# Splitting the rotated q and k, and spreading v, on GpSimd instead of ScalarE and VectorE (attention batches 2 to 8)

## The reference

```python
q  = split_heads(layernorm(x) @ Wq, 16)          # 16 heads of 16 features
kv = split_heads(layernorm(x) @ Wkv, 16)         # keys and values are the same tensor
q  = (q * cos + rotate_half(q) * sin) * 16 ** -0.5
kv = kv * cos + rotate_half(kv) * sin
# 8 segments of 64 rows; segment s attends to segments s-1 and s, causally inside s
attn = softmax(where(causal, -max, q_s @ concat(kv_{s-1}, kv_s).T))
out  = merge_heads(attn @ concat(kv_{s-1}, kv_s)) @ Wo + bo     # segment 0: itself only, Wo0 and bo0
x = x + out
```

## Time and profile before

| | us |
|---|---|
| median of three runs | 2736.92 |
| the profiled execution | 2742.4 |
| its span, first to last instruction | 2740.4 |
| attention of batches 1 to 7, with the next one prepared beside each | about 56 to 436 |
| attention of batch 8 | 436 to 484 |
| feed-forward, recurrence, feed-forward | 484 to 2740 |

### The profile page before, as it was taken

How to read it: one execution, slowest core, us unless ns; L and a number is a source line. 1 busy time by engine, 2 the same in 40 slices (tenths; PEclk the granted TensorE clock), 3 DMA queues, 4 the chain that set the end, 5 groups by cost and what they waited for, 6 DMA issues and landing times. The chain is left out here.

```text
span 2740.4 us, 46536 instructions
## 1 busy us (share of the span) xinstructions
PE 1995.3 (73%) x12353; PEld 1597.9 (58%) x12353; DVE 2238.8 (82%) x5728; ACT 1569.2 (57%) x4695; POOL 912.4 (33%) x1522
## 2 busy tenths in 40 slices
PE   6888888885877767677777777777777764344687
PEld 3555555453777666667676666666666664233344
DVE  6888876786069999999999999999999999993576
ACT  4888786665455555555555555555555554443566
POOL 0000000110034545545444445444444454541111
PEclk8999997898987776777767777777767676665799
DMA  5001000000000000000000000000000000000000
GB/s 163 16 19 30 16 16 12 1 1 1 0 1 0 0 0 0 0 1 0 0 1 0 0 0 1 0 0 0 0 0 1 0 0 1 0 0 0 8 24 31
DMA packets 14211, 23.57 MB, mean 9 GB/s; under 512 B 1280, under 2 KB 12032, under 8 KB 13824
## 3 DMA queue, kind: packets, MB, share of 16 engines
q1 hardware_dynamic: 14080, 21.97, 2.8%
HBM read 12.27 MB, written 4.19 MB: 6 GB/s over the span
## 5 line engine op out<-in xcount | busy, mean ns | idle before, releaser
L1560 POOL TENSOR_TENSOR wu<-U,stg 128x256 f32<-128x256 f32 x512 | 318.5, 622 | 853.4 <-DVE U L1485 853.4
L700 PE MATMUL bank<-U,ident 128*128 128x128 f32 x2080 | 471.1, 398 | 120.4 <-ACT go L962 102.5
L700 PEld LDWEIGHTS bank<-U,ident 128*128 128x128 f32 x2080 | 434.5, 251 | 162.6 <-issue 73.4
L763 PE MATMUL bank<-stack,tm 128*128 128x64 f32 x1792 | 349.1, 384 | 218.6 <-ACT tm L899 218.6
L1099 ACT ACTIVATE xs<-U 128x256 f32<-128x256 f32 x512 | 213.5, 417 | 469.4 <-DVE U L1485 467.7
L763 PEld LDWEIGHTS bank<-stack,tm 128*128 128x128 f32 x1792 | 337.6, 293 | 238.4 <-issue 238.4
L1435 DVE TENSOR_REDUCE pn<-xs 128x32 f32<-128x512 f32 x512 | 351.2, 686 | 29.4
L1517 POOL TENSOR_TENSOR kv<-stg 128x256 f32<-128x256 f32 x513 | 318.6, 621 | 1.7
L686 PE MATMUL bank<-wcat,yT 128*128 x1024 | 301.5, 455 | 3.0 <-issue 3.0
L1028 ACT ACTIVATE small<-pn 128x16 f32<-128x16 f32 x513 | 110.8, 216 | 306.1 <-DVE pn L1435 306.1
L686 PEld LDWEIGHTS bank<-wcat,yT 128*128 128x128 f32 x1024 | 247.2, 252 | 31.1 <-issue 18.4
(11 more groups left out here) (180 smaller groups left out, 3719.5 us busy)
## 6 DMA issues: line engine op xcount, KB each, us to landing
out_x<-x SPq DMA_DIRECT2D x8, 512.0 KB, 2.9
x<-in_x SPq DMA_DIRECT2D x1, 3584.0 KB, 16.4
Vs<-V SPq DMA_DIRECT2D x8, 384.0 KB, 4.7
Vs<-V SPq DMA_DIRECT2D x8, 288.0 KB, 3.3
lane<-in_lanes SPq DMA_DIRECT2D x8, 256.0 KB, 3.2
wcat<-in_wcat SPq DMA_DIRECT2D x1, 1792.0 KB, 14.8
wraw<-in_w_up SPq DMA_DIRECT2D x1, 1024.0 KB, 18.5
wraw<-in_w_down SPq DMA_DIRECT2D x1, 1024.0 KB, 11.5
```

Of the source, the lines that this page charges most:

```text
L700: last = pe.matmul(rsum.rearrange("p (t i) -> p t i", i=HD), ident[:, :], steps[:, :, :, j], start=(j == 0), stop=(j == HD - 1))
L763: last = pe.matmul(bank[3 + g][:, e * CH:(e + 1) * CH], tm[:, g * (PB // 2) + e, :, :].rearrange("p a c -> p (a c)"), stack[:, :], start=T ...
L1560: pool.tensor_tensor(ij(wu[:, :]), ij(U[:, half if j else 1 - half, (j - 1) % STEPS, :]), col(stg[:, half, j, TW, :]), ALU.mult).then_inc( ...
```

## The change

For batches 2 to 8, ScalarE no longer calls its `split_heads` and VectorE no longer calls its own. GpSimd does all five instructions of a tile: the high half of q, the low half of q, the high and the low half of k, and last the spread of v. It waits for `zr` of the tile and for the TensorE transposes that free `qk4`; between a high half and its subtraction it waits for its own result. GpSimd's loop over the batches is written out, and its `pow` of batch b + 3 stands ahead of the tiles of batch b + 2. VectorE gets one wait more ahead of its addition into `zr`: that the values of two tiles before have been spread. The first batch stays as it was.

```diff
@@ ScalarE, batch()
-                    if more and (w - 6) % 3 == 0 and 6 <= w < 18:
-                        split_heads(nxt, par_n, (w - 6) // 3)
@@ VectorE, rotate()
                 dve.wait_ge(A["lo"], p * (2 * NT) + 2 * max(u - 1, 0))
+                dve.wait_ge(A["v"], p * NT + max(u - 1, 0))
@@ VectorE, batch()
-                    if more and (w - 7) % 3 == 0 and 7 <= w < 19:
-                        split_heads(nxt, (w - 7) // 3)
@@ GpSimd
-            with pool.Fori(2, B) as q:
-                pool.wait_ge(A["ve"], q + 1)
-                pool.tensor_tensor(sd[:, 0, :], vv[:, 0, :], halves[:, 0, :], ALU.pow).then_inc(A["sd"], 1)
+
+            def split_heads(p, u):
+
+                pool.wait_ge(A["zr"], p * NT + u + 1)
+                pool.wait_ge(A["qt"], p * (2 * NT) + 2 * max(u - 1, 0))
+                for w, (hi, lo) in enumerate(((slice(0, 4, 2), slice(1, 4, 2)), (slice(0, 2), slice(2, 4)))):
+                    z = zr[:, u % 2, w, :, :].unsqueeze(2).to_broadcast([P, H, 2, HD])
+                    pool.tensor_copy(qk4[:, u % 2, w, :, hi, :], z).then_inc(A["hiq"], 1)
+                    pool.wait_ge(A["hiq"], p * (2 * NT) + 2 * u + w + 1)
+                    pool.tensor_tensor(qk4[:, u % 2, w, :, lo, :], z, qk4[:, u % 2, w, :, hi, :],
+                                       ALU.subtract).then_inc(A["lo"], 1)
+                if u == 0:
+                    pool.wait_ge(A["vs"], p * 32)
+                pool.tensor_copy(V[:, p % 2, u, :, 0:3 * HD].rearrange("p j (e d) -> p j e d", d=HD)[:, :, 0:3:2, :],
+                                 zr[:, u % 2, 1, :, :].rearrange("p (j e) d -> p j e d", e=2)).then_inc(A["v"], 1)
+
+            for b in range(B - 1):
+                if b < B - 2:
+                    pool.wait_ge(A["ve"], b + 3)
+                    pool.tensor_tensor(sd[:, 0, :], vv[:, 0, :], halves[:, 0, :], ALU.pow).then_inc(A["sd"], 1)
+                for u in range(NT):
+                    split_heads(b + 1, u)
```

## The result

The changed kernel takes 2757.66 us, the median of six runs (2755.02 to 2758.56); the kernel before, run beside it on the same chip, takes 2737.35 (2732.44 to 2745.72, six runs). The ratio is 1.0069, with a 95% interval of 1.0051 to 1.0087: slower by some 20 us, and more than the 0.5% that a measurement of this kernel can tell from no change. The profiled execution took 2757.66 us with a span of 2755.8, 15.4 more than the span before, whose execution was itself 5 us above its median.

A forecast was written before the change was run, and what follows sets the result against it. No engine is full; a ring of TensorE, VectorE and ScalarE bounds the attention. +0.3 us (gain eaten by the wait for Vs), +1 for lane loads and +3.5 for the shared port gave +5, 2742 us; range 2724 to 2763.

The forecast's parts named there:

- the likeliest case: Whole kernel: the forecast itself, +5 us to 2742 us, within 0.5% of no change; chance 0.45.
- blocked for whole instructions: VectorE and GpSimd holding each other up for entire instructions, at tile 1's scan and Vs's landing: +14 us, 2751; chance 0.15.
- long 16-bit operations: GpSimd's splits taking about 1.9 us for each of four, so Vs lands late: +26 us, 2763; chance 0.18.
- TensorE's transposes of q and k: After the rotation: some 10 us available, q and k need 2.3 and 4.6 us from GpSimd, so no wait.
- VectorE's new wait for V: Ahead of the addition into zr: asks for V of two tiles, six steps, ago; costs nothing.
- The shared port: VectorE and GpSimd holding each other up at tile 1's scan: 0 to 1.1 us a period, taken as 0.5; +3.5 us.
- The relief: Splits taken off ScalarE and VectorE: only tile 3 gains, 0.85 us a period, 6.0 us over seven periods.
- the other three tiles: Tiles 0, 1 and 2 of a period: removing their splits gains nothing, as the engines wait for TensorE there.
- the ring closes up: Attention: two of four splits stand on the path, a period gains 2.7 us; -19 us, 2718; chance 0.10.
- The V path: Tile 3 to step 18's first product with Vs: GpSimd does V last, Vs lands late, gain eaten; +0.3 us in sum.

The follow-up runs named there:

- small operations: Changed kernel with GpSimd's five operations on one head of q and k and two of v, the rest left out: 2724.2 us beside 2736.3, ratio 0.996.
- memsets: Kernel before, plus four GpSimd memsets of 1024 f32 elements a tile, writing SBUF and reading none of it: ratio 1.0005.

## Why the prediction was right or wrong

**Right.** The kernel became slower, not faster, and 2757.7 lies in the range of 2724 to 2763. But the likeliest case said within 0.5%, at 2742, and that was wrong by 16 us; slower by over 0.5% had 0.26. The rival *blocked for whole instructions* (2751, with 0.15) was the nearest in its mechanism. The rival *long 16-bit operations* (2763) was a little nearer in its number, but its mechanism did not occur. That the sum of too small a cost and too small a gain still fell into the range is in part luck. TensorE's transposes of q and k were covered as argued, ScalarE fell to the 38 us foreseen, and VectorE's new wait for V costs nothing.

**The step that failed: "The shared port".** It had +3.5 us, 0.5 a period, up to 1.1, and looked at one place only: the scan of tile 1, ahead of `oT_a`. The runs show 22 us for it without relief and 30 with it, by the ratios. It went wrong in its count, not in its mechanism. There are four scans a period, one behind every `zr`, and all lie in GpSimd's five instructions; I counted that of tile 1, and that of tile 3 only through V. `xn` and the bias addition were not counted at all; a longer `xn` by itself turned out to be cheap, but at tile 3 the two make up most of the 1.25 us by which the maxima came later. The rule of the Trainium skill that I quoted (SBUF — State Buffer, "Who interferes with whom") bears on every VectorE instruction with two SBUF inputs beside a GpSimd one that reads, and the trace agrees: 1.95 us for a subtraction that takes 1.16, 1722 ns for a scan of 1265. I applied it to one instruction a period, where it should have been applied to each of the list behind `zr`: a list of VectorE's instructions in GpSimd's 5 us, each with its excess, was to be had from the same timeline. The rule as I quoted it speaks of two inputs; `xn` has one tensor input and was stretched as well. The scan on 32 partitions, which I held against the rival, is no protection: it was stretched by 36%.

**The relief was undersized.** I found 0.85 us a period on the path, 6 us in all, and held the other three tiles for covered. With the small operations it is 12 us by the medians, twice my 6. In the profiled executions the attention of that kernel ends 19.9 us sooner than before (450.06 for 469.91), of which some 5 may be the execution before, which was 5 us above its median; its five periods are 51.8, 51.7, 50.4, 51.7 and 52.0 us. Periods of under 53 us were my sign that more of the splits was on the path than I found, and once the reads are taken away they are there. So the 19 us of *the ring closes up* cannot be excluded as the size of the relief.

**The V path was oversized.** I expected the gain to be eaten by the wait for Vs, late by about 1 us in the first three periods. There was one wait, of 1.6 to 1.9 us. Without blocking a tile takes GpSimd 0.69 + 1.10 + 0.75 + 1.16 + 0.40 = 4.1 us from start to start, and with it about 5, against my 5.2 plus 0.6. The terms in it: a subtraction 1.16 us (I took 1.10), a cast 0.61 (0.95), the V copy 0.40 (0.62). The rival *long 16-bit operations* falls with them: its sign, single GpSimd operations near 2 us, did come (1.95), but for a subtraction that was blocked.

**The range** held for the wrong reason: its upper end came from the long 16-bit operations, which did not happen.

## What to carry to other kernels

Work given to GpSimd is not free for VectorE: before moving it, list what VectorE does in the time in which GpSimd will read, and count each instruction there with SBUF inputs as possibly longer; here `xn` grew by up to 0.7 us a time and the scan by 0.46, with GpSimd instructions of 0.6 to 1.2 us beside them. Where it matters, price it with dummies on GpSimd beside the unchanged kernel. Then place the GpSimd reads beside VectorE's instructions on PSUM, with an explicit wait on the last SBUF instruction ahead of them: here that turned +19 us into -11.

## What the hardware showed that was not expected

- `xn`, one SBUF tensor with two scalars a partition, 407 ns for 256 elements, is held up by GpSimd's reads (903 ns) and by its memsets (1100 ns). The scan, with two inputs, is held up by reads (1722 to 1777) and not by memsets (1260). The bias addition is like the scan: 560 beside the reads, 425 beside memsets.
- The waiting is in the recorded durations, on the engine that came second: a cast 1.46 us instead of 0.61 behind a scan, a subtraction 1.95 instead of 1.16. A group's mean over its minimum shows it, no wait does.
- GpSimd's casts to f16 are cheap: 0.61 us for 512 elements, about what 256 elements of a two-input f32 multiplication cost it (0.62).
